# A seam built early and an expert loop run two ahead, in a two-layer kernel of gated attentions and experts

## The reference

```
x = x + tanh(g_xattn[0]) * causal_attention(layernorm(x), ctx)      # one head of 256
x = x + tanh(g_ffn[0])   * capacity_experts(layernorm(x))           # 256 -> 1024 -> 256, gelu
x = x + tanh(g_xattn[1]) * dilated_attention(layernorm(x), ctx)     # 16 heads of 16, 3 branches
x = x + tanh(g_ffn[1])   * choice_experts(layernorm(x))             # 256 -> 682 -> 256, silu
```

## Time and profile before

| what | value |
|---|---|
| time, median of 3 runs | 938.09 us (936.34 to 939.6) |
| profiled execution: time / span | 939.1 / 937.4 us |
| mean granted clock of TensorE | 0.833 |
| TensorE busy | 654.0 us, 70% |
| VectorE busy | 528.3 us, 56% |
| ScalarE busy | 427.8 us, 46% |
| POOL busy | 338.0 us, 36% |

### The profile page before, as it was taken

One profiled execution on the slowest core, in us unless ns is written; L12 is line 12 of the kernel. 1 busy time (PEld: TensorE's weight loads), 2 busy tenths in 40 slices (PEclk: granted clock), 3 DMA queues, 4 the chain that ended last, 5 costly groups with the idle time before them and its releaser, 6 DMA issues. The chain is left out here.

```text
span 937.4 us, 15352 instructions
## 1 busy us (share of the span) xinstructions
PE 654.0 (70%) x4856; PEld 486.4 (52%) x4856; DVE 528.3 (56%) x1701; ACT 427.8 (46%) x847; POOL 338.0 (36%) x473
## 2 busy tenths in 40 slices
PE   3999983145999999999324877788877301757755
PEld 3888872123877778777212444455445200545543
DVE  0467753625656666564025578877755387555651
ACT  1344430034567775576112546566555110564652
POOL 1244431053653466452212444544433201323422
PEclk9999995557999999999755788998888555787877
DMA  5132321334453455441311212332100110435332
GB/s 174 45 124 84 121 91 45 125 94 134 103 136 82 121 130 113 126 78 23 50 40 41 70 42 80 92 93 62 45 25 34 71 59 14 146 89 153 89 86 23
DMA packets 74955, 78.66 MB, mean 84 GB/s; under 512 B 8101, under 2 KB 66513, under 8 KB 74641
## 3 DMA queue, kind: packets, MB, share of 16 engines
q1 hardware_dynamic: 62305, 62.11, 21.0%
q0 software_dynamic: 10928, 15.57, 9.7%
q10 hardware_dynamic: 1664, 0.27, 0.2%
HBM read 54.99 MB, written 22.94 MB: 83 GB/s over the span
## 5 line engine op out<-in xcount | busy, mean ns | idle before, releaser
L1650 DVE CUSTOM_DVE_ANT_0 c_sn<-c_ps_s,k_mask 128x128 f32<-128x128 f32 (+1 forms) x256 | 75.8, 352 | 57.7 <-PE c_ps_s L1788 57.6
L1174 PE MATMUL b_ps_y<-b_w2h,b_hh 128*128 128x256 f16 x320 | 87.3, 273 | 4.5 <-DVE b_xl L1050 4.2
L924 POOL DMA_INDIRECT res<-b_y,b_s_idx x40 | 72.7, 1816 | 42.4 <-ACT b_y L966 30.8
L1174 PE MATMUL b_ps_y<-b_w2l,b_hh 128*128 128x256 f16 x320 | 87.2, 273 | 0.0
L1174 PE MATMUL b_ps_y<-b_w2h,b_hl 128*128 128x256 f16 x320 | 87.2, 273 | 0.0
L910 POOL DMA_INDIRECT b_xg<-rows,b_g_idx x40 | 43.8, 1094 | 119.7 <-DVE b_g_idx L1068 110.0
L1482 POOL TENSOR_SCALAR_AFFINE_SELECT c_pr<-c_pr 128x512 f32<-128x512 f32 x64 | 42.9, 671 | 111.0 <-ACT c_pr L1541 110.0
L1041 DVE TENSOR_TENSOR b_hl<-b_h,b_hh 128x640 f16<-128x640 f32 x64 | 52.8, 825 | 36.9 <-ACT b_hh L946 36.7
L1816 PE MATMUL c_ps_v<-c_pr,k_vx 128*64 128x256 f32 (+1 forms) x512 | 64.0, 377 | 5.5 <-POOL c_pr L1482 4.9
L1139 PE MATMUL b_ps_h<-b_xh,b_w1h 128*128 128x320 f16 x256 | 57.1, 305 | 12.7 <-ACT b_h L941 9.3
L941 ACT ACTIVATE b_h<-b_ps_h,b_b 128x640 f32<-128x640 f32 x64 | 50.1, 784 | 18.8 <-DVE b_hl L1041 11.6
(11 more groups left out here) (382 smaller groups left out, 1812.2 us busy)
## 6 DMA issues: line engine op xcount, KB each, us to landing
b_w<-in_L_ffn_W_dram SPq DMA_DIRECT2D x16, 1024.0 KB, 5.6
d_w<-in_L_ffn_W_up_dram SPq DMA_DIRECT2D x8, 682.0 KB
d_w<-in_L_ffn_W_down_dram SPq DMA_DIRECT2D x8, 640.0 KB
k_ks<-kT SPq DMA_DIRECT2D x48, 64.0 KB, 2.5
c_qs<-q SPq DMA_DIRECT2D x48, 64.0 KB, 2.3
rows<-a_rows SPq DMA_DIRECT2D x8, 264.0 KB, 2.5
rows<-c_rows SPq DMA_DIRECT2D x8, 264.0 KB, 2.2
a_x_in<-in_x_dram SPq DMA_DIRECT2D x8, 256.0 KB, 3.0
```

The costliest lines, as they stand in the source:

```text
L924: pool.indirect_dma_start(out=dram["res"], out_offset=bass.IndirectOffsetOnAxis(ap=s_idx[u][:, j:j + 1], axis=0), in_=y[:, j, :], in_offse ...
L1174: last = pe.matmul(ps_y[(j + CT) % 2][:, 0:D], a, b[:, f, :], start=(f == 0 and k == 0), stop=(f == FC - 1 and k == 2))
L1650: dve.tensor_tensor_reduce(sn[r][:, a:b], ps_s[:, r, a:b], mask[:, a:b], -1.0, 3.0e38, ALU.add, ALU.min, mx[g % 2][:, q, r, j:j + 1]).then ...
```

## The change

Two rewrites in one.

**The seam.** (a) The loop of the first attention is written out. (b) The keys and values for the second attention leave the steps: the turned contexts of all 8 sequences are kept, in the space of the weights that are no longer needed (`w_all`), and the products are done behind the last scores, in a tail whose order is written by hand. (c) Into this tail come the tables of the capacity experts: positions of 8 experts, each with half a key or value product behind it, the turn of the biases, the indices of experts 0 and 1 (`marks`, `high_parts`, `low_parts`, `rows_of`), the high and low halves of the first expert's `W1`, and the gather of its rows; loads of its `W1`, `W2` and `b2` go out in steps 1 and 3. The tiles are allocated by `capacity_tables` before the stage, and `dilated_tiles` after it. (d) The capacity stage begins with step -1 without slots, gathers expert 1 there, and VectorE's `second_attention_members` stands at the start of step E - 2. The count of fallen tokens is made last in the tail.

**The choice experts.** The loop is written out over all experts. TensorE does hidden(e + 1) before down(e), then turns the rows of e + 2 and builds the index of e + 3; VectorE marks for e + 4. Rows have a bank of their own (`ps_r`), indices five tiles, gathered rows four, `hh`, `hl` and `y` two. `W_down` has two staging tiles (both zeroed by POOL at the start), `W_up` is loaded and split once per group instead of once per expert. Casts of `hidden` cover a pair of chunks. Biases and gates are read in place, the scatter uses the gather's index, and ScalarE loads the table of Silu ahead by one activation on `warm`.

```diff
-        w = {n: sb(n, [P, C, D]) for n in names}
+        w_all = sb("w_all", [P, len(names), C, D])
+        w = {n: w_all[:, i] for i, n in enumerate(names)}
+        cT = [w_all[:, n] for n in range(B)]
...
 
-            def run(eng):
-                step(0, 0, True, False, False)
-                step(1, 1, True, True, False)
-                with eng.Fori(0, B // 2 - 2) as i:
-                    step(i * 2 + 2, 0, True, True, True)
-                    step(i * 2 + 3, 1, True, True, True)
-                step(B - 2, 0, True, True, True)
-                step(B - 1, 1, True, True, True)
-                step(B, 0, False, True, True)
-                step(B + 1, 1, False, False, True)
+            def run():
+                for n in range(B):
+                    step(n, n % 2, True, n >= 1, n >= 2)
             return run
...
+                if n == 1:
+                    sp.dma_start(b1_in[:], ins["L0_ffn_b1"].rearrange("e (c p) -> (e c) p", p=P)).then_inc(s_ldb1, 16)
+                    sp.dma_start(w1[:], ins["L0_ffn_W1"][0].rearrange("(c p) f -> p c f", p=P)).then_inc(s_w1, 16)
+                if n == 3:
+                    sp.dma_start(w2[:], ins["L0_ffn_W2"][0].rearrange("(c p) d -> p c d", p=P)).then_inc(s_w2, 16)
+                    sp.dma_start(b2[:], ins["L0_ffn_b2"].partition_broadcast(P)).then_inc(s_b2, 16)
...
+            key_parts(0)
+            gates_of(B - 2, 0)
+            key_parts(1)
+            scale_of(B - 1, 1)
+            key_parts(2)
+            key_parts(3)
+            gates_of(B - 1, 1)
+            for n in range(4, B):
+                key_parts(n)
+            pool.wait_ge(s_gi, 1)
+            for u in range(2):
+                pool.wait_ge(s_rst[u], 16 * B // 2)
+            apart(pool, s_pass)
+            for j in range(CT):
+                pool.indirect_dma_start(
+                    out=xg[0][:, j, :], out_offset=None, in_=dram["rows"],
+                    in_offset=bass.IndirectOffsetOnAxis(ap=g_idx[0][:, j:j + 1], axis=0)).then_inc(s_g[0], 16)
...
+            pipeline(step)()
+            keys(0)
+            residual_turned(B - 2, 0)
+            second_exp(B - 2, 0)
+            keys(1)
+            keys(2)
+            residual_normalised(B - 1, 1)
+            keys(3)
+            residual_turned(B - 1, 1)
+            second_exp(B - 1, 1)
+            for n in range(4, B):
+                keys(n)
+            act.wait_ge(s_w1, 16)
+            for high in up:
+                act.activation(high[1], high[0], ACT.Copy, scale=WS0).then_inc(s_wh1, 1)
...
+            values(0)
+            top_two(B - 2, 0)
+            probabilities_turned(B - 1, 1)
+            matches(B - 2, 0)
+            gate_values(B - 2, 0)
+            residual(B - 1, 1)
+            values(1)
+            values(2)
+            dve.wait_ge(s_ecst, 8)
+            dve.tensor_copy(free[:], one_row[:]).then_inc(s_free, 1)
+            values(3)
+            top_two(B - 1, 1)
+            matches(B - 1, 1)
+            dve.wait_ge(s_gate, 2 * B - 1)
+            for e in range(E):
+                eligible(e)
+                if e == 0:
+                    gate_values(B - 1, 1)
+                if e == 1:
+                    dve.wait_ge(s_pb1, 1)
+                    dve.tensor_copy(b1T[:], ps_i[:, BT:BT + E * FC]).then_inc(s_b1T, 1)
+                if e in (2, 4, 6):
+                    values(e // 2 + 3)
+                overflowing(e)
...
+            high_parts(0)
+            low_parts(0)
+            values(7)
+            rows_of(0)
+            high_parts(1)
+            low_parts(1)
+            for k, low in enumerate(up):
+                dve.wait_ge(s_wh1, k + 1)
+                dve.scalar_tensor_tensor(out=low[2], in0=low[0], scalar=WS0, in1=low[1], op0=ALU.mult,
+                                         op1=ALU.subtract).then_inc(s_wl1, 1)
+            rows_of(1)
+            dve.tensor_scalar(fallen[:], free[:], -1.0, 1.0, ALU.mult, ALU.add).then_inc(s_fell, 1)
...
+            pipeline(step)()
+            keys(0)
+            values(0)
+            residual_turn(B - 2, 0)
+            probability_turn(B - 1, 1)
+            logits(B - 2, 0, B - 1)
+            keys(1)
+            mixed(B - 1, 1, B)
+            values(1)
+            keys(2)
+            values(2)
+            keys(3)
+            residual_turn(B - 1, 1)
+            values(3)
+            logits(B - 1, 1, B - 1)
+            keys(4)
+            values(4)
+            pe.wait_ge(s_ecst, 8)
+            pe.wait_ge(s_ldb1, 16)
+            pe.transpose(ps_i[:, BT:BT + E * FC], b1_in[:], ident[0:E * FC, 0:E * FC]).then_inc(s_pb1, 1)
+            keys(5)
+            for e in range(E):
+                positions(e)
+                n, r = 5 + (e + 2) // 4, e % 2
+                if e in (0, 1, 4, 5):
+                    if r == 0:
+                        after(pe, s_v, n, 2)
+                    last = half_product(bank_v[n % 2], cT[n], wvT1, r)
+                    if r == 1:
+                        last.then_inc(s_pv, 1)
+                else:
+                    if r == 0:
+                        after(pe, s_kT, n, 2)
+                    last = half_product(bank_k[n % 2], wkT1, cT[n], r)
+                    if r == 1:
+                        last.then_inc(s_pk, 1)
+            values(7)
+            token_rows(0)
+            token_rows(1)
...
-                step(-2, 0, True, False, False)
-                step(-1, 1, True, True, False)
+                step(-1, 1, False, True, False)
...
-                if slots:
+                if slots or isinstance(e, int) and e == -1:
...
+                if isinstance(e, int) and e == E - 2:
+                    second_attention_members()
...
-                if isinstance(e, int) and e == -1:
-                    second_attention_members()
...
+        g_idx = [sb(f"g_idx{u}", [P, CT], I32) for u in range(5)]
+        xg = [sb(f"xg{u}", [P, CT, S.ROW]) for u in range(4)]
...
-            pool.memset(w2[:], 0.0).then_inc(s_fill, 1)
+            for u in range(2):
+                pool.memset(w2[u][:], 0.0).then_inc(s_fill, 1)
...
+            load_up(0)
+            load_down(0)
+            load_down(1)
+            for e in range(E):
+                if e % 2 == 0 and group(e) + 1 < G:
+                    sp.wait_ge(s_wl1, group(e) + 1)
+                    load_up(group(e) + 1)
+                if e + 2 < E:
+                    sp.wait_ge(s_wl2, e + 1)
+                    load_down(e + 2)
...
+            for e in range(-3, E):
+                if e + 3 < E:
+                    gather(e + 3)
+                if e >= 0:
+                    scatter(e)
...
+            act.wait_ge(s_warm, 1)
+            act.activation(warm[:], warm[:], ACT.Silu)
...
+            for e in range(-1, E):
+                if e + 1 < E:
+                    for p in range(PAIRS):
+                        hidden(e + 1, p)
+                    if e + 2 < E:
+                        rows_high(e + 2)
+                    down_high(e + 1)
+                    if e % 2 == 1 and group(e + 3) < G:
+                        up_high(group(e + 3))
+                if e >= 0:
+                    scaled(e)
...
+
+            marked(0)
+            found(0)
+            marked(1)
+            up_low(0)
+            found(1)
+            marked(2)
+            rows_low(0)
+            for e in range(-1, E):
+                if e + 4 < E:
+                    marked(e + 4)
+                if e + 1 < E:
+                    hidden_low(e + 1, 0)
+                if e >= 0:
+                    down_low(e)
+                if e + 1 < E:
+                    hidden_low(e + 1, 1)
+                if e >= 0 and e % 2 == 0 and group(e + 2) < G:
+                    up_low(group(e + 2))
+                if e + 1 < E:
+                    hidden_low(e + 1, 2)
+                if e + 2 < E:
+                    rows_low(e + 2)
+                if e + 3 < E:
+                    found(e + 3)
+                if e >= 0:
+                    biased(e)
...
+            found(0)
+            found(1)
+            turned(0)
+            for e in range(-1, E):
+                if e + 1 < E:
+                    hidden(e + 1)
+                if e + 2 < E:
+                    turned(e + 2)
+                if e + 3 < E:
+                    found(e + 3)
+                if e >= 0:
+                    down(e)
```

More of the change, by code:

```diff
@@ new lines, in keys, with values, half_product @@
+            def keys(n):
+                after(pe, s_qT, B - 1)
+                after(pe, s_kT, n, 2)
+                product(bank_k[n % 2], wkT1, cT[n]).then_inc(s_pk, 1)
+            def values(n):
+                after(pe, s_vp, B - 1)
+                after(pe, s_v, n, 2)
+                product(bank_v[n % 2], cT[n], wvT1).then_inc(s_pv, 1)
+            def half_product(bank, lhs, rhs, r):
+                for c in range(C):
```

(4 more changed lines are left out.)

988 lines of the change are left out of this document (504 added, 484 removed).

## The result

The changed kernel takes **881.03 us** (median of 4 runs, 880.62 to 881.46), the kernel before beside it 938.85 us (936.34 to 943.64): a ratio of 0.9379, 95% interval 0.934 to 0.9417. Forecast were 868.5 us with a range of 850 to 893, so the direction and the range for eight in ten held. The range of my own case, 860 to 877, was missed, and the gain was 57.8 us where 69.6 were forecast. The profiled execution has a span of 879.3 us and a mean clock of 0.860 (0.833 before).

The account below looks back on a forecast made before the run. TensorE bounds first attention and capacity experts, small dependent steps the seam, waits between engines the last stage. Gains 23.4 + 11.8 + 34.4 = 69.6 us off 939.1 give 869.5, predicted as 868.5 us; eight-in-ten range 850 to 893.

Parts of the forecast that it names:

- my own case: Whole kernel: the main forecast, 868.5 us, with its own range 860 to 877 and chance 0.48.
- The steps: First attention: a steady step falls from 13.48 to 11.65 us as key and value products leave; last scores at 117.0.
- The tail: Last scores to first hidden product of the capacity experts: 63.8 us, so that product starts at 180.8 instead of 204.2.
- 8 us more for the tail: Tail: by the skill's port-lock rule the last four key splits could hold the chain; kernel end near 877.
- The stall: Capacity experts, 212.3 to 224.2 us: VectorE's wait on POOL's fills goes, -11.8 us.
- The front of the last stage: Ahead of the choice experts: 1.9 us more, from a second memset of w2 (1.37) and marks and w1 low part (0.5).
- The experts of the last stage: Choice experts: 11.2 us each, TensorE waiting about 2 us in one of two iterations; 93.6 us in sum.
- the first attention that doesn't gain: Rival, chance 0.13: steps stay near 13.5 us because VectorE's work is a chain, products add a tail; 879.5 us.
- the last stage waits more: Rival, chance 0.20: gather waits over 2 us bring the slow clock back, 13.5 us per expert; 884 us, range 877 to 895.
- The barrier did not hold the seam: Rival, chance 0.02: the time stays where it is because the barrier, not a chain, held the seam.
- The dense case: Rival, chance 0.15: first-attention steps at 10.5 us, last-stage experts at 10.2; 854 us, from 846 to 858.
- the worst case: Bounds: steps staying at 13.48 us, 11.0 less gain, and experts at 13.5, 16 less; given as 899.5 without a rival.

Follow-up runs that it names:

- filled_steps: Changed kernel plus one product of eight matmuls that nobody reads, ahead of the router's logits in each of the six steady steps of the first attention; 877.36 us.
- keys_in_steps: Changed kernel with the key products of sequences 0 to 5, their biases, splits and stores back in the first attention's steps 2 to 7; 886.47 us.
- gathers_apart: Changed kernel with POOL waiting, in the last stage, until expert 0's rows have landed before issuing expert 1's gather; 877.22 us.
- clears_late: Changed kernel with the 14 semaphores that cross the first seam released at the end of the last stage, not the second; 881.74 us in one run.
- choice_only: Kernel before with only the last stage's rewrite, all other stages as before; 910.32 us, ratio 0.9696 to the kernel before.
- pad_only: Changed kernel with POOL zeroing only the last chunk of the two staging tiles of the down weights; 876.18 us.
- the last kernel: Changed kernel with sooner upward-weights load, small fills and later key copies, plus group 1's upward-weights load waiting for expert 0's rows; 868.49 us over 6 runs.

## Why the prediction was right, and where its sizes were off

**The steps.** I gave a steady step 11.65 us from a chain that the products had covered. At the upper level of the clock it takes 11.3 to 12.0, and TensorE does wait for the turned residual, 0.65 us in each of the six. The term that was mis-sized is the clock: I took the 1.00 of the earlier trace rows over to a step with holes. Two of six steps fell to 0.87 in the profiled execution, four of six in others; the six took 72.7 us where I had 69.9. filled_steps shows that a product in the last of the holes keeps the clock up; keys_in_steps, with longer waits and the clock at 1.00, shows that idle time alone is not the reason. The last scores come at 116.8 us, 117.0 forecast, but by luck: from the first turn on the stage took 88.4 us where I had 86.3, and this execution began 2.3 us earlier than that of before (starts between 27 and 31.7 us occur in all kernels).

**The tail.** 64.8 us against 63.8. In its terms: 24.6 (25.5 forecast) to the first position, 13.8 (16) for the eight positions, 7.4 (6) to the index, 14.0 (11.3) to the first turn, 5.0 (5) to the first hidden product. For the positions I had counted eight intervals of 1.48 us where eight positions have seven, 1.3 too much; the rest is about as priced: POOL's key splits stretched four of VectorE's instructions by 2.2 us in sum (2.7 forecast), and about 1 us is left for the three value additions (1.2). The last split hit the index instead, where VectorE's two instructions on the marks took 0.59 and 1.20 us for expert 0 and 0.23 and 0.24 for expert 1. The 14.0 are the barrier: [7.55 <-PEq L77] ends a wait on TensorE's own queue, and the last packet of the gather had landed at 174.6 us, 2.0 before. I had laid the barrier under the gather's flight; it ended last. The Trainium skill (SBUF — State Buffer, "Who interferes with whom") says that VectorE and GpSimd exclude one another on their shared ports for a whole instruction; by that rule I had estimated 8 us more for the tail. The trace agrees with the rule where the two meet, and not with my count of meetings. Here a VectorE instruction that takes 0.18 us elsewhere lasts to the end of POOL's:

```profile
149.89 1.17 POOL L445 TENSOR_TENSOR a_kl<-a_kT,a_kh 128x512 f16<-128x512 f32 x1
149.95 1.15 DVE L710 TENSOR_TENSOR_SCAN a_cum<-a_one_row,a_elig 128x16 f32<-128x16 f32 x1
```

But the last four splits take 7.0 us, and only six of VectorE's instructions were stretched in the positions and the index, by 3.5 us in sum: the first of these splits was nearly over at the first position, and the others met the chain for part of their length only.

**The stall.** Gone in its full size: 12.2 us less from the first hidden to the first down product (11.8 forecast). That the stretch as a whole gained only 6.4 has two reasons. From the first down product to the last matmul it took 222.0 us against 218.1 before; but in the profiles of gathers_apart and clears_late it took 218.1 and 218.2, and in choice_only, with the old code, 219.8: that is scatter between executions. And the seam behind it takes 21.2 to 22.0 us in eleven of the twelve profiles with the new first seam (20.3 in filled_steps) and 19.5 in the two with the old one. These 2 us do belong to the change. About half lie ahead of the issue of the third stage's first load, and their cause stays open; it is not the release of the semaphores. The other half lie in the landing of this load, beside a packet of an instruction queue.

**The third stage.** Its +2.0 us are a stretch at the lower clock that falls in other places in other executions.

**The front of the last stage.** +4.2 us, 1.9 forecast. The fill of 1.37 us and what goes with it is about as priced (pad_only takes 1.7 to 2.3 back). The rest is a transfer that I had not looked at: with the low half of the down weights moved from this place, the one of the upward weights is ready before the rows have landed, and the 682 KB that it releases go out at 768.3 us, in front of the rows; before the change they went out at 795.2, one us before the rows were used. The kernel with the additional wait shows it: with the small fills and this wait, the stretch from the last router product of the third stage to the first hidden product of the fourth is 62.6 us, 62.8 before the change.

**The experts of the last stage.** 94.6 us, 93.6 forecast, and still the step failed: I had every second iteration wait 2 us for the gather. The gather ends TensorE's waits twice in that stretch, 3.5 us in sum. What made the iterations of 12 and 14 us is the load of the upward weights, behind a wait in SP's queue for another tile, and in the longer one the clock of 0.88 behind it. That the sum came out within 1 us is luck. My rule had been to name what is queued behind each wait, and I had done so for POOL and VectorE but not for SP. TensorE alone needs less than my 10.15 us: 9.4 once nothing waits. Its matmuls start 0.11 us apart in the timeline, which makes 7.9 for 72 of them, where I had taken the 8.72 that the earlier trace rows give as busy in a window.

**The rivals.** Nearest in number lay the first attention that doesn't gain (879.5 us), and it did gain: 88.4 us from the first turn to the last scores where it was 104.2. That the last stage waits more (884 us) is next, and its mechanism, a wait on the gather, is refuted. The barrier did not hold the seam, though it ends the last 2.0 us of the wait for the first rows. The dense case is what the last experts of the last stage come to, 9.4 to 9.5 us apart. In the bounds one sum is wrong: the two losses named there, 11.0 and 16 us, put the worst case at 895.5 us and not at 899.5.

## What to carry to other kernels

When a change makes several queues run ahead, write out the queue of transfers too: for each load, what the queue waits for ahead of it, when its tile is really free, and whose transfer it meets. Here one reordered loop of loads was worth 7.3 to 7.5 us, an eighth of what the whole change gained. Work that is taken out of a dense stretch should be priced at both levels of the clock; and if the stretch then drops to the lower one, something may be put back for nothing, if it brings no wait into any of the other queues.

## What the runs showed of the hardware that was not expected

In the steady steps of the first attention, TensorE had waits of 0.25, 0.2 and 0.65 us in 11.5 us, and the granted clock fell to 0.87 in a third to two thirds of them; with the last of these waits filled it stayed at 1.00 in all six, and with key products in the same place it did so too, beside waits of up to 1.7 us. Which step is hit changes between executions of one kernel, and so does the whole: a stage with the same code took 261.4 to 265.9 us, and the six executions of the last kernel lie between 860.4 and 872.9 us. Differences of 3 us between kernels with such stretches are read from their places in the trace, not from their times.
